# A selective scan and an attention block: layer norms and q/k norms by token tile, four batches written out, VectorE's guests moved to mid-row

## The reference, cut to what matters

```
# part 1
h, gate = adaln(x, c)                            # layer norm, scale, shift
x = x + gate * (ssm(h, fwd) + flip(ssm(flip(h), bwd)))
h, gate = adaln(x, c)
x = x + gate * ((silu(h @ w1) * (h @ w2)) @ w3)
# ssm: xs, z = split(h @ in_w); xs = silu(xs); proj = xs @ xproj_w
#      dt = softplus(proj[:512] + dt_bias); Bm, Cm = the other 64 + 64 columns
#      state = state * exp(dt * A) + (dt * xs) * Bm  over 512 tokens, for 512 channels x 64 states
#      y = sum over states of state * Cm, + xs * D;  return (y * silu(z)) @ out_w
# part 2
x1 = ln(x) * (scale1 + 1) + shift1
q, k, v = x1 @ qkv_w + bias, 16 heads of 16      # q_bias, none for k, v_bias
q = l2norm(q) * exp(min(scale_mul, log 100)); k = l2norm(k)
x = x + (softmax(q k^T) v @ proj_w + proj_b) * gamma1
x2 = ln(x) * (scale2 + 1) + shift2
x = x + (gelu(x2 @ fc1_w + fc1_b) @ fc2_w + fc2_b) * gamma2
```

## Time and profile before

| what | value |
|---|---|
| median of 3 runs | 3528.84 us (3526.27 to 3528.93) |
| the profiled execution's own time | 3529.55 us |
| its span, first to last instruction | 3527.8 us |
| mean granted TensorE clock | 0.963 of full speed |
| busy: PE / DVE / ACT / POOL | 3275.1 / 2823.1 / 2734.3 / 2487.5 us |

### The profile page before, as it was taken

The page is one execution under the profiler, slowest core; times in us unless marked ns, Lnnn a source line. Parts: engine busy times, 40 slices in busy tenths (PEclk is TensorE's granted clock), DMA queues, the critical chain, the costliest instruction groups (busy, mean ns, idle before and its releaser), DMA issues.

```text
span 3527.8 us, 68244 instructions
## 1 busy us (share of the span) xinstructions
PE 3275.1 (93%) x22944; PEld 2605.5 (74%) x22944; DVE 2823.1 (80%) x3001; ACT 2734.3 (78%) x4713; POOL 2487.5 (71%) x1103
## 2 busy tenths in 40 slices
PE   7999999988799999998979999999798999999888
PEld 4778888864488888886458788888546888888744
DVE  2899999956299999995639999999455999999653
ACT  1989999952498999993349999999146999999523
POOL 1789999950098999993019999999203999999600
PEclk9999999997999999999889999999989999999989
DMA  3221212100111121110011211212002211111000
GB/s 127 82 68 49 70 55 68 60 26 13 48 65 62 55 70 54 63 67 25 1 59 60 68 53 66 67 57 67 13 1 75 66 56 61 60 55 57 29 13 7
DMA packets 56732, 186.83 MB, mean 53 GB/s; under 512 B 6577, under 2 KB 12721, under 8 KB 55473
## 3 DMA queue, kind: packets, MB, share of 16 engines
q1 hardware_dynamic: 56370, 182.26, 15.3%
HBM read 179.08 MB, written 3.16 MB: 52 GB/s over the span
## 4 chain that ended last, share of the span: by engine, by line
POOL 47%; issue 25%; PE 24%; DVE 3%; DMA 1%; POOLq 0%; ACT 0%; SPq 0%; DVEq 0%; ACTq 0%
POOL states L531 45%; PE bank L993 3%; PE bank L860 3%; PE bank L851 3%; PE bank L900 2%; PE bank L1012 2%; PE bank L1074 2%; PE bank L1024 2%; PE bank L852 1%; PE bank L774 1%; PE bank L800 1%; POOL part L514 1%; PE bank L963 1%; PE bank L736 0%; PE bank L944 0%
## 5 line engine op out<-in xcount | busy, mean ns | idle before, releaser
L531 POOL TENSOR_TENSOR states<-states,c_rows 128x1024 f32<-128x1024 f32 x1024 | 2401.5, 2380 | 566.3 <-DMA c_rows<-c_spill 293.0
L1226 DVE TENSOR_TENSOR_SCAN states<-decay,bank 128x512 f32<-128x512 f32 x2048 | 2336.4, 1201 | 152.8 <-PE bank L852 106.1
L643 ACT ACTIVATE decay<-dt,a_log 128x512 f32<-128x512 f32 x2048 | 1305.5, 710 | 0.0
L860 PE MATMUL bank<-ident,states 128*128 128x128 f32 x8192 | 1240.5, 275 | 34.6 <-POOL states L531 11.9
L851 PE MATMUL bank<-ident,inflow_tok 128*128 128x128 f32 x6144 | 1070.3, 283 | 63.1 <-DVE states L1226 54.3
L637 ACT ACTIVATE inflow_tok<-dtx_tok,b_tok 128x512 f32<-128x512 f32 x1536 | 995.3, 712 | 134.7 <-PE bank L852 134.2
L860 PEld LDWEIGHTS bank<-ident,states 128*128 128x128 f32 x8192 | 952.5, 142 | 76.7 <-POOL states L531 73.4
L851 PEld LDWEIGHTS bank<-ident,inflow_tok 128*128 128x128 f32 x6144 | 686.7, 141 | 361.6 <-issue 127.1
L852 PE MATMUL bank<-b_diag,dtx_tok 128*128 128x128 f32 x4096 | 794.5, 276 | 0.0
L852 PEld LDWEIGHTS bank<-b_diag,dtx_tok 128*128 128x128 f32 x4096 | 621.3, 192 | 0.0
L638 ACT ACTIVATE b_diag<-ident,b_tok 128x128 f32<-128x128 f32 x512 | 199.3, 389 | 0.0
(11 more groups left out here) (143 smaller groups left out, 1968.6 us busy)
## 6 DMA issues: line engine op xcount, KB each, us to landing
c_rows<-c_spill SPq DMA_DIRECT2D x256, 512.0 KB, 3.7
xproj_w<-in_xproj_w SPq DMA_DIRECT2D x32, 320.0 KB, 4.3
in_w<-in_in_w SPq DMA_DIRECT2D x16, 512.0 KB, 4.8
in_w<-in_fc_w SPq DMA_DIRECT2D x8, 512.0 KB, 5.3
xproj_w<-in_w SPq DMA_DIRECT2D x8, 512.0 KB, 5.0
xproj_w<-in_fc_w SPq DMA_DIRECT2D x4, 1024.0 KB, 4.8
y_gated<-in_mod_w SPq DMA_DIRECT2D x1, 2048.0 KB, 7.6
x_ahead<-in_x SPq DMA_DIRECT2D x4, 512.0 KB, 5.1
```

What stands on the lines that cost most here:

```text
L531: pool.tensor_tensor(pair, pair, c_row, ALU.mult).then_inc(weighed, 1)
L643: act.activation(decay[:, r % SLOTS * KI + k, :], dt[:, d, k, :], ACT.Exp, scale=a_neg[:, d, k, s:s + 1]).then_inc(decay_ready, 1)
L860: last = pe.matmul(banks[KI + t][:, k * P:(k + 1) * P], states[:, r % SLOTS * KI + k, t * P:(t + 1) * P], ident[:], is_transpose=True, sta ...
L1226: dve.tensor_tensor_scan(states[:, slot, time], decay[:, slot, time], banks[k % INFLOW_BANKS][:, time], 0.0, ALU.mult, ALU.add).then_inc(s ...
```

## The change

1. **Batches written out.** All engines run `for b in range(B): batch(b, b == B - 1)`. Indices and semaphore targets are constants; the semaphore `wait_over`, which only register targets needed, goes.
2. **Guests in mid-row.** DVE scans tiles 0 and 1, does `prepare` and `look_ahead`, then scans tiles 2 and 3.
3. **The look-ahead's norm pieces** (L1209) become `scalar_tensor_tensor`, with `rstd` as a broadcast second tensor.
4. **Residuals and layer norms by token tile**, one bank per tile; two ACT pieces of 128 columns for each tile in place of one of 512 on ACT and on DVE. proj's and FC2's biases are added by a matmul of one row.
5. **QKV** of a tile starts once its own layer norm is ready; it alternates between two q/k banks. The K copy is ACT's. The chain root, maximum, reciprocal, scale, padding goes by tile; q's scales and k's -1 stand in one tile `qk_scale`.
6. **Head groups**: only the first query and key group is turned before the scores, the others behind scores 1, 4 and 7, into banks 6 and 7. All copies but the first are ACT's. The leading scores use 6 banks.

```diff
-LEAD_BANKS = 7
+LEAD_BANKS = 6
+LN_BANK = 6
+QK_BANK = 4
+TURN_BANK = 6
+LATE_TURN_AT = {1: 1, 4: 2, 7: 3}
...
-            with pe.Fori(0, B - 1) as b:
-                batch(b, False)
-            batch(B - 1, True)
+            for b in range(B):
+                batch(b, b == B - 1)
...
 # ACT, ln
+                def shift(t):
+                    act.wait_ge(ln_turned, n + t + 1)
+                    for f in range(KD):
+                        act.activation(h_t[:, f, t * P:(t + 1) * P], banks[LN_BANK + t % 2][:, f * P:(f + 1) * P], ACT.Identity,
+                                       bias=mod[:, i, SHIFT, f, b:b + 1], scale=mod[:, i, SCALE, f, b:b + 1]).then_inc(ln_ready, 1)
+                for t in range(TT):
+                    act.wait_ge(ln_var, n + t + 1)
+                    act.activation(std[:, t:t + 1], var_eps[:, t:t + 1], ACT.Sqrt).then_inc(ln_std, 1)
+                    if t:
+                        shift(t - 1)
+                shift(TT - 1)
...
 # ACT, batch
+                for t in range(TT):
+                    act.wait_ge(q_ready, b * TT + t + 1)
+                    act.activation(qk[:, t, D:2 * D], banks[QK_BANK + t % 2][:, D:2 * D], ACT.Copy).then_inc(k_ready, 1)
+                    if t:
+                        root(t - 1)
+                root(TT - 1)
...
 # PE
+            def residual_tile(t, lhs, rhs, steps, bias=None):
+                to = banks[t][:, 0:D]
+                if bias is not None:
+                    pe.matmul(to, ident[0:1, 0:1].to_broadcast([1, P]), row_b[0:1, bias, :], start=True, stop=False)
+                for c in range(steps):
+                    last = pe.matmul(to, lhs(c, t), rhs(c), start=(c == 0 and bias is None), stop=(c == steps - 1))
+                last.then_inc(res_mm, 1)
...
+                for t in range(TT):
+                    for k in range(KI):
+                        last = pe.matmul(banks[t][:, 0:D], y_chan[:, 1, k, t * P:(t + 1) * P], out_w[:, 1, k, :],
+                                         start=False, stop=(k == KI - 1))
+                    last.then_inc(res_mm, 1)
...
                 for t in range(TT):
+                    if t == TT - 1:
+                        ln_turn(b, 2, 0)
+                    residual_tile(t, lambda c, t: ab[:, c, t * P:(t + 1) * P], lambda c: w3[:, c, :], KH)
+                for t in range(TT):
+                    if t + 1 < TT:
+                        ln_turn(b, 2, t + 1)
+                    ln_wait(b, 2, t)
+                    if t > 1:
+                        pe.wait_ge(k_ready, b * TT + t - 1)
...
+                turn_heads(0)
                 pe.wait_ge(v_ready, (b + 1) * TT)
-                pe.wait_ge(qk_t_ready, (b + 1) * 2 * NG)
+                pe.wait_ge(q_t_first, b + 1)
...
                 for u in range(LEAD):
                     scores(u)
+                    if u in LATE_TURN_AT:
+                        turn_heads(LATE_TURN_AT[u])
...
 # DVE
+            def residual_ln(b, i, g, eps):
                 for t in range(TT):
+                    n = (b * 3 + i) * TT + t
+                    residual(b, i, g, t)
+                    dve.wait_ge(res_ready, (b * RES + i) * TT + t + 1)
+                    dve.bn_stats(stats[:, t, :], x_of[i + 1][:, t, :]).then_inc(ln_stat, 1)
+                    if t:
+                        normalise(b, i, t - 1)
+                    dve.wait_ge(ln_stat, n + 1)
                     dve.bn_aggr(mean_var[:, t, :], stats[:, t, :]).then_inc(ln_aggr, 1)
+                    dve.wait_ge(ln_aggr, n + 1)
+                    dve.tensor_scalar(var_eps[:, t:t + 1], mean_var[:, t, 1:2], eps, None, ALU.add).then_inc(ln_var, 1)
+                normalise(b, i, TT - 1)
...
-                    dve.tensor_scalar(x_norm[:, t, :], x_ahead[:, t, :], mean_var[:, t, 0:1], rstd[:, t:t + 1],
-                                      ALU.subtract, ALU.mult).then_inc(ahead_norm, 1)
+                    dve.scalar_tensor_tensor(x_norm[:, t, :], x_ahead[:, t, :], mean_var[:, t, 0:1],
+                                             rstd[:, t:t + 1].to_broadcast([P, D]), ALU.subtract,
+                                             ALU.mult).then_inc(ahead_norm, 1)
...
-                    scan_row(b, r)
-                    if d == 1 and s == 0:
-                        gate_rows(b, 0)
+                    scan_row(b, r, range(0, PAIR))
...
                         prepare(b * 2 + d + 1, 1 - d, s)
                     if d == 0 and not last:
                         look_ahead(b + 1, s)
+                    scan_row(b, r, range(PAIR, KI))
+                    if d == 1 and s == 0:
+                        gate_rows(b, 0)
...
+                for t in range(TT):
...
+                dve.wait_ge(qk_turned, b * 2 * NG + 1)
+                dve.tensor_copy(q_t[:, 0, :], banks[TURN_BANK]).then_inc(q_t_first, 1)
```

More of the change, by code:

```diff
@@ L503, in _ @@
                                        ALU.mult).then_inc(diag_ready, 1)
+            pool.memset(qk_scale[:, H:2 * H], -1.0).then_inc(sign_ready, 1)
             pool.memset(minus_half[:], -0.5).then_inc(half_ready, 1)
@@ L556, in batch @@
                 for t in range(TT):
-                    pool.wait_ge(qk_ready, b * TT + t + 1)
+                    pool.wait_ge(q_ready, b * TT + t + 1)
+                    pool.wait_ge(k_ready, b * TT + t + 1)
                     pool.tensor_tensor(qk_sq[:, t, :], qk[:, t, :], qk[:, t, :], ALU.mult).then_inc(sq_ready, 1)
-            with pool.Fori(0, B - 1) as b:
-                batch(b, False)
-            batch(B - 1, True)
+            for b in range(B):
+                batch(b, b == B - 1)
         @block.scalar
@@ L703, in batch @@
                     act.activation(gelu_h[:, m, :], banks[m], ACT.Gelu, bias=fc1_b[:, m:m + 1]).then_inc(fc1_ready, 1)
-            with act.Fori(0, B - 1) as b:
-                batch(b, False)
-            batch(B - 1, True)
+            for b in range(B):
+                batch(b, b == B - 1)
         @block.tensor
@@ L894, in scan_row @@
                             look_ahead(b + 1, s, b * 2 + 1)
-            def residual_rows(lhs, rhs, steps):
-                for t in range(TT):
-                    for c in range(steps):
-                        last = pe.matmul(banks[t // 2][:, (t % 2) * D:(t % 2 + 1) * D], lhs(c, t), rhs(c),
-                                         start=(c == 0), stop=(c == steps - 1))
-                    if t % 2:
-                        last.then_inc(res_mm, 1)
+            def residual_tile(t, lhs, rhs, steps, bias=None):
[5 more added lines that the diff above has]
+                last.then_inc(res_mm, 1)
             for at in range(NS):
@@ L1136, in add_up @@
-            def add_up(b, i, n, tiles):
-                dve.wait_ge(res_gated, n + 1)
-                dve.tensor_tensor(x_of[i + 1][:, tiles, :], x_of[i][:, tiles, :], gated[:, tiles, :],
-                                  ALU.add).then_inc(res_ready, 1)
-                if i + 1 < RES:
-                    dve.wait_ge(res_ready, n + 1)
-                    for t in range(tiles.start, tiles.stop):
-                        dve.bn_stats(stats[:, t, :], x_of[i + 1][:, t, :]).then_inc(ln_stat, 1)
@@ new lines, in residual, with normalise @@
+            def residual(b, i, g, t):
+                n = (b * RES + i) * TT + t
+                dve.wait_ge(res_mm, n + 1)
+                dve.tensor_tensor(gated[:, t, :], banks[t][:, 0:D], gate[:, g, :], ALU.mult).then_inc(res_gated, 1)
+                dve.wait_ge(res_gated, n + 1)
+                dve.tensor_tensor(x_of[i + 1][:, t, :], x_of[i][:, t, :], gated[:, t, :], ALU.add).then_inc(res_ready, 1)
+            def normalise(b, i, t):
+                n = (b * 3 + i) * TT + t
+                dve.wait_ge(ln_std, n + 1)
+                dve.reciprocal(rstd[:, t:t + 1], std[:, t:t + 1]).then_inc(ln_rstd, 1)
+                dve.wait_ge(ln_rstd, n + 1)
+                dve.tensor_scalar(x_norm[:, t, :], x_of[i + 1][:, t, :], mean_var[:, t, 0:1], rstd[:, t:t + 1],
+                                  ALU.subtract, ALU.mult).then_inc(ln_norm, 1)
@@ L1339, in batch @@
                 dve.tensor_copy(o_t[:, 0, :], banks[0]).then_inc(o_t_ready, 1)
-                residual(b, 2, GAMMA1, PROJ_B)
-                ln(b, 3, x_att, EPS_LN)
-                residual(b, 3, GAMMA2, FC2_B)
-            with dve.Fori(0, B - 1) as b:
-                batch(b, False)
-            batch(B - 1, True)
+                residual_ln(b, 2, GAMMA1, EPS_LN)
+                for t in range(TT):
+                    residual(b, 3, GAMMA2, t)
+            for b in range(B):
+                batch(b, b == B - 1)
 def kernel(**inputs):
```

223 lines of the change are left out of this document (89 added, 134 removed).

## The result

The changed kernel takes **3509.06 us** (median of 5 runs, 3505.29 to 3515.47) against 3526.27 (3522.01 to 3528.93) for the kernel before beside it: ratio 0.9952, 95% interval 0.9937 to 0.9966. It is faster, as forecast, but by 17 us and not by 113, and the time lies outside the range of 3384 to 3460. The profiled execution's span is 3503.5 us.

The account below looks back on a forecast made before the run. In the scan no engine was saturated but all near it, with DVE's idle time worth the same in time. Scan 54.4, batch starts 12 and behind the scan 47 us gave 113.4 off 3529.55: 3416 us, range 3384 to 3460.

Parts of the forecast that it names:

- The scan's guests: Scan: DVE's guests run beside PE's matmul between tiles, instead of both being paid one after the other; gain 44.0 us.
- rival b: POOL paces the scan: half of the 44 us becomes DVE waits, 3438 us, or all of it, 3460; chance 0.13.
- The norm pieces: Look-ahead in the scan: the new form takes 0.46 us a piece beside POOL; gain 10.4 us over three batches.
- Rival (a): Look-ahead's norm pieces stay blocked beside POOL, twice per look-ahead, giving 10 us back: 3426 us; chance 0.27.
- Batches written out: Batch starts: removing two loop jumps gains net 12 us, while the written-out batch's scans keep the same pace.
- Behind the scan: Stages behind each scan: per batch 2.35 and 9.8 us gained, 0.5 lost; 47 us over four batches.
- w3's end to the first score: Second residual through QKV to the first score: gains of 8.0 and 6.0 us per batch.
- The lead: Leading scores: transposes interrupting them give back 3.0 us, and 6 banks for 7 another 1.2, per batch.
- Third residual: Projection and third norm: bias becomes a matmul pass; slower per-tile DVE work cancels its early start: 0 us.
- (c): Per-tile transposes keep PE at 2.4 GHz through layer norms; MLP and FC1 save 21 us: 3395 us; chance 0.08.
- (d): Slower scan: DVE stands in mid-row until ACT's product for its guest is there: 3584 us; chance 0.04.
- (e): The written-out program brings nothing at batch starts, the wait being for C rows: 3428 us; chance 0.03.

Follow-up runs that it names:

- the experiment: Kernel before, loop kept, with only DVE's guests moved from behind scan 4 to between scans 2 and 3 of a row: 3523.81 us, ratio 0.9991.
- chosen places: Changed kernel with guests behind the fourth scan in rows 3, 11, 19, 26 and 47, in mid-row elsewhere: 3489.33 us, ratio 0.9896 to the kernel before.

## Why the prediction was wrong

**The scan's guests, 44 us forecast, 3 to 6 measured.** The failed step is "the two are paid one after the other". It holds in row 14, which I had read: PE has no piece in row 15. It holds in 6, 38 and 46 too, and mostly in 22. In the other six of my 11 rows (8, 16, 34, 41, 43, 50) the row behind has a piece, and the guest at the row's end already ran beside it. And rows 3, 11, 19, 26 and 47, with a guest and no piece of their own, covered their neighbour's and lose that: five gained, five lost, 11 covered before and 11 after. The 11 shorter and 11 longer rows of the experiment are these. One more row of each timeline would have shown it. POOL (rival b) did not decide this; where places were chosen, it let 20 us through.

**The norm pieces, 10.4 us forecast, none measured.** The failed step is the choice of 0.46 "nearest to the short row". Rival (a), at 0.27, is what happened: 1.20, 0.59, 0.59, 2.33. What these four take less than before (4.71 against 5.29) comes from their place in the row, not from the form. The guests that never stretched read one tensor from PSUM, a difference that I had named and set aside. The Trainium skill, page "SBUF — State Buffer", section "Who interferes with whom", has the rule that a DVE instruction with two SBUF inputs contends with a GpSimd one that reads SBUF. Here the trace agrees: the new form, whose second input is a broadcast column, took 0.48 us alone and was held until 0.28 us behind the end of POOL's product in every case with one under way at its start.

**Batches written out, 12 forecast, 8 measured.** Right in mechanism. The term was sized without what a written-out wait costs when it is late (5.04 to 5.10 us a row); "the scans of the written-out batch have the same pace, so nothing" is the step. The trace before already showed it: in the preparing half of the fourth, written-out batch ten rows last 5.10 us, where the looped batches have 5.04. I had compared the pace of scans and not uncovered rows. The jump itself fits the Trainium skill, page "Runtime: NRT & Kernel Launch", section "Instruction fetch mechanics", by which a branch taken out of the instructions already fetched waits for a fetch; it names no time, and 8.09 us is the trace's. No run here parts a fetch from the rest of the jump.

**Behind the scan, 47 forecast, 14 in the profiled execution, 3 by comparison of kernels.** Of the 14, 4 came with the written-out batches alone, and about 5 belong to the third batch, whose projection escaped the half clock in this execution. With the guests at the row's end, where all four projections had it, the four stretches last 746.8 us, 3.4 less than with written-out batches alone. The kernel with written-out batches alone and the changed kernel with its guests at the row's end differ only in this and the norm's form, 0.9977 against 0.9968: 3 us, with intervals that don't part it from nothing. By steps, second batch:
- First layer norm: 3.4 for 2.35. Right in mechanism; the sum has 3.0 us behind PE's end where its own terms give 2.85.
- w3's end to the first score: 11.1, less 0.7 for a slower w3, for 14.0. QKV kept its full clock and ended 12.6 behind w3, 11.9 forecast; the unit chain gave 4.0 for 6.0.
- The lead: 6.9 lost for 4.2. Stalls of 2.65, 1.09 and 0.20 stand where I had 1.3, 0.9 and 0.8: PE's first turns run at half clock there (1.97 us for eight, against 1.10 later). Moving them gave 4.1 back.
- Third residual: 4.5 lost for 0. This is the largest miss. I priced its bias at full clock and under DVE's cover; the half clock, which before had come behind the projection, sat on it, so each tile's bias took 1.22 us (0.44 in my sum) and each pass of the projection twice its time, and PE became the bound (3.15 us a tile, for DVE's 2.15, and DVE waits 1.02 for it). The bias moved into the waits gave 22 us in all.
- Fourth residual: 1.75 lost for 0.5. PE's bias passes take 2.47 and not 1.7, 0.62 for a tile at full clock.

Of the rivals, (c), that the clock stays up, is not borne out: 0.9 us came back in the MLP and 0.6 in FC1, against 5 lost in the projection, but written-out batches alone, with the old layer norms, gave 0.8 in the MLP, and had raised the mean granted clock from 0.963 to 0.968 of the 0.969 after. (d) did not occur: in the whole run DVE's guests that ACT feeds wait 19.2 us for it, 19.3 before. (e) is out for DVE, whose 8.09 fell to 0.46. For POOL it holds in part: its first product of the third batch still waits for the C rows and comes 9.2 us behind the residual's end, 12.5 before and 7.0 in the written-out batch that I took as the model. After the late turns, the moved biases and the filled pauses the four stretches last 703.0 us, 51 less than before. That this is near the 47 forecast is luck: these three edits (12, 22 and 9 us) were not in the prediction, and they confirm none of its terms.

What stays open: what makes the clock fall in one batch and not in the same stage of the next. The projection took 11.12 in three batches and 6.02 in one, and which one it is changes: the third in the changed kernel, the first with chosen places, none with guests at the row's end. The transposes moved it, but no run shows a rule. It also blurs every comparison of a few microseconds here, since executions of one kernel differ by up to some 10 us, the slower ones at a lower mean clock (the changed kernel's: 3505.29 us at 0.969 and 3515.47 at 0.965).

## What to carry to other kernels

Before a guest is moved, list for every row what each engine does in that row **and the next**, and count covered pieces before and after, not gaps that the new place would cover. A bias that moves onto PE belongs into a wait that PE has anyway, and small work inserted into a pipelined lead belongs behind as many units as the stall it makes is long. An operation held up while another engine works was mended here by its place in that engine's rhythm; the one change of form that was tried did nothing.

## What the runs showed of the hardware

A DVE instruction with two SBUF inputs, issued 0.3 us into a POOL product, took 2.33 us and ended 0.28 behind it; issued 0.3 before a product's end it took 0.59 in place of 0.48. A loop's jump left DVE 8.09 us without an instruction; written out it is 0.46 or less. But a piece of PE in the way delays a scan by 0.63 us in written-out code and 0.57 in the loop. In these traces the clock fell behind thin stretches of PE, though not behind each: after 7.5 us with PE busy for 4.54 it was 0.50 for the next 11.5, although PE was then busy without a pause. Idle transposes of no use made the kernel 9 us faster.
